# Wide bf16 filler matmuls behind the first layer's second and third norm and at the end of every pass

## The chip, the cores and the metric

The kernel runs on one core of a Trainium2 chip, in one launch. The metric is the device time in microseconds. Three runs of the kernel before took 2702.28, 2705.74 and 2709.91 us (median 2705.74). TensorE's matmul side is called PE in the profile, its weight loads PEld; DVE is VectorE, ACT ScalarE, POOL GpSimd, SP the engine that issues the transfers.

## The reference, cut to what matters

Four layers are applied one after the other to `x` of 32 sequences, 128 tokens and 128 features, with a context of the same shape:

- layer 0: a transformer decoder block, 16 heads of 64: causal self attention, residual and layer norm (`ln1`); cross attention to the context, residual and layer norm (`ln2`); feed-forward of 512 with relu, residual and layer norm (`ln3`);
- layer 1: a small attention with 16 heads of 8, masked per query;
- layer 2: an encoder block and a decoder block with linear attention, 8 heads of 16;
- layer 3: a small attention, a norm and projection to `U`, then a recurrence over the 128 tokens, `s = silu(s @ A.T) + u_t`, whose states are projected and added to the result.

```python
x = _layer_norm(ca + residual, ln2_g, ln2_b)
residual = x
h = jax.nn.relu(x @ ffn_w1 + ffn_b1)
x = _layer_norm(h @ ffn_w2 + ffn_b2 + residual, ln3_g, ln3_b)
```

## The kernel before, in words

**Passes.** The 32 sequences are worked on in 8 passes of 4 (`G = 4`, `GT = 512` tokens). In each pass a main stream computes layer 0 of its four sequences, and a side stream computes layers 1 to 3, up to `U`, of the four sequences of the pass before. Pass 0 has set-up work in place of the side stream. After pass 7 the side stream runs once alone (about 2313 to 2582 us of the span), and then the recurrence of all 32 sequences runs in one scan of 127 steps, to 2702 us.

**Order.** Every engine has its own program, written by the same generators: `MAIN_STEPS` is the list of the main stream's steps, and `interleave` (called from `passes`, line 423) takes one main step and then as many side steps as `SIDE_PACE` says are due. So the order on each engine is fixed, and an engine that waits holds up all that is behind it, of both streams. The main steps at the end of a pass are

```python
steps += [[("ln2", "y")], [], [], [("ln2", "norm")], [("ln2", "n")], []]
steps += [[("ffn", 0), ("ffn", 1)], [("ffn", 2), ("ffn", 3)], []]
steps += [[("ln3", "y")], [], [], [("ln3", "norm")], [("ln3", "n")]]
```

**A norm.** Item `y`: PE sums the projection and the residual into PSUM bank 0 (`sums`, line 654, matmuls of line 660). DVE takes the moments (lines 1159 to 1165), POOL the power -0.5 (line 546), DVE writes the normalised tokens to `main_normed` in four instructions (`normalise`, line 1172). Item `n`: PE turns them to feature-major with four transposes (`turn4`, line 648), and DVE applies gain and bias (line 1185) into `xT_a` (after `ln2`) or `xT_b` (after `ln3`). After `ln2` come the four feed-forward matmuls (line 652, `ps<-xT_a,w_f`), whose results ACT and DVE take in turn. After `ln3`'s `n`, PE waits until DVE has taken the turned tokens (`wait_emptied`, line 761).

**The hand-over.** DVE then copies `xT_b` to `x_side`, `cT` to `c_side`, makes the side's query mask (lines 1269 to 1272) and the masks of the next pass (lines 1203 to 1209). PE turns the next input (`x_in`), makes the side's first three projections (lines 652 and 800), turns the context (`c_in`) and, once DVE has copied that to `cT` (line 1224), starts the next self attention with `w_qkv_sa`.

**PSUM.** The main stream uses banks 0 to 4, the side stream 5 to 7. Bank 3 holds the attention's outputs (`o`) and one of the value products; it is read out before `ln2`'s `y` begins.

**The matmuls.** fp32 operands take two PE instructions for each matmul of the program; bf16 takes one. `scores` adds the mask with one bf16 matmul of 512 columns (line 698). The scan has a local helper `keep_busy(width)` (line 965) that multiplies `ident_h` (a bf16 identity) with `width` columns of `mask_ca` into bank 5 in each step, 512 or 256 wide.

Of the kernel before, what the change touches and what calls it, by code (L numbers as in the profile page):

```python
# [50 lines left out]
def main_steps():  # L51
# [8 lines left out]
    def attention(tag):  # L60
        for s in range(UNITS + 3):
# [11 lines left out]
            if tag == "sa" and s % 2 and s < 2 * G:  # L73
# [14 lines left out]
MAIN_STEPS = main_steps()  # L88
NO_FILL = ("scale", "norm")
IDLE = 1  # L90


SIDE_PACE = ([8] * (2 + IDLE) + [4] * (SMALL["l1"][0] * G + 2) + [3] * 37
             + [4] * (SMALL["l3"][0] * G + 2) + [4] * 7)
# [154 lines left out]
def build_program(nc, I, out):  # L249
    with ExitStack() as ctx:  # L250
        def sb(name, shape, dt=F32):
            return ctx.enter_context(nc.sbuf_tensor(name, shape, dt))
# [4 lines left out]
        ps = ctx.enter_context(nc.psum_tensor("ps", [128, 8, 512], F32))  # L257
# [3 lines left out]
        ident_h = sb("ident_h", [128, 128], BF16)  # L261
# [40 lines left out]
        mask_ca = sb("mask_ca", [128, G, T], BF16)  # L302
# [92 lines left out]
        def bank(st, name):  # L395
            return ps[:, st.bank[name], :]
# [5 lines left out]
        def wait_emptied(eng, i, st, name):  # L402

            by = st.by[name]
            eng.wait_ge(emptied[st, by], i.at(st.total[by], st.rank[name]))
# [8 lines left out]
        def wait_all_emptied(eng, i, st, names):  # L414

            last = {}
            for name in names:
                by = st.by[name]
                last[by] = max(last.get(by, 0), st.rank[name])
            for by, rank in last.items():  # L420
                eng.wait_ge(emptied[st, by], i.at(st.total[by], rank))
# [77 lines left out]
        def _(pool):  # L499
# [63 lines left out]
            def side(i):  # L563
# [22 lines left out]
                yield  # L586
                for _ in range(IDLE):
                    yield
# [50 lines left out]
        def _(pe):  # L639
            mm = nc.tensor.matmul  # L640
            pe.wait_ge(consts_ready, n_const[0])
            pe.wait_ge(loaded_first, n_first[0])
            nc.tensor.transpose(ps[:, 5, 0:NCOLS], col_rows[:, :], ident[0:NCOLS, 0:NCOLS]).then_inc(setup_filled, 1)

            def turn4(st, name, src):

                for b in range(G):
                    last = nc.tensor.transpose(bank(st, name)[:, b * 128:b * 128 + 128], src(b), ident[:, :])  # L648
                last.then_inc(filled[st], 1)

            def one(st, name, lhs, rhs):
                mm(bank(st, name)[0:lhs.shape[-1], :], lhs, rhs, start=True, stop=True).then_inc(filled[st], 1)  # L652
# [14 lines left out]
            def token(x, b):  # L667
                return x[:, b * T:b * T + T]

            def before_filling(i, item, *needed):  # L670

                held = [MAIN.before[item]] if MAIN.before[item] is not None else []
                wait_all_emptied(pe, i, MAIN, held + list(needed))

            def project(i, item):
                tag, kind, n = item[:3]
                x = {"sa": xT["a"], "ca": xT["b"] if kind == "q" else cT}[tag]
                if item == ("ca", "v", 0, 0):
                    pe.wait_ge(loaded_ca, n_ca[0])

                needed = {("sa", "k", 0): [("in", 0), ("in", 1)], ("ca", "q", 0): [("ln1", "n")]}
                before_filling(i, item, *needed.get(item, []))
                if kind == "v":
                    one(MAIN, item, token(x, item[3]), w_qkv[tag][:, 2, n * 512:n * 512 + 512])
                else:
                    one(MAIN, item, w_qkv[tag][:, "qk".index(kind), n * 128:n * 128 + 128], x[:, :])

            def scores(i, item):

                tag, _, u = item  # L690
                c, b0 = u // 2, 2 * (u % 2)
                before_filling(i, item, (tag, "k", c), (tag, "q", c))
                for n in range(2):
                    at = slice((b0 + n) * T, (b0 + n) * T + T)
                    mm(bank(MAIN, item)[:, n * 256:n * 256 + 256], queries[:, c % 2, at], keys[:, c % 2, :, at],  # L695
                       start=(n == 0), stop=False, skip_group_check=True)
                mask = (mask_sa if tag == "sa" else mask_ca)[:, b0:b0 + 2, :]
                mm(bank(MAIN, item), ident_h[:, :], mask.unsqueeze(2).broadcast_to([128, 2, 2, T]),  # L698
                   start=False, stop=True, skip_group_check=True).then_inc(filled[MAIN], 1)

            def turn(i, item):
                tag, _, u = item
                before_filling(i, item)
                pe.wait_ge(scaled, i.at(2 * UNITS, u + 1 + (0 if tag == "sa" else UNITS)))
                for h in range(4):
                    last = nc.tensor.transpose(bank(MAIN, item)[:, h * 128:h * 128 + 128],  # L706
                                               probs[:, u % 3, h * 128:h * 128 + 128], ident[:, :])
                last.then_inc(filled[MAIN], 1)
# [14 lines left out]
            def main(i):  # L723
                for step in MAIN_STEPS:
                    for item in step:
                        tag, kind = item[:2]
                        if tag == "in":

                            if kind == 0:
                                pe.wait_ge(group_in, i.at(48, 48))  # L730
                            turn4(MAIN, item, lambda b: (c_in if kind else x_in)[:, b, :])
                        elif tag == "ffn":
                            before_filling(i, item, ("ln2", "n"))
                            one(MAIN, item, w_f1[:, kind * 128:kind * 128 + 128], xT["a"][:, :])
                        elif kind in ("q", "k", "v"):
                            if item == ("sa", "v", 0, 0):

                                pe.wait_ge(masks_taken, i.at(1, 1))
                            project(i, item)
                        elif kind == "s":  # L740
                            scores(i, item)
                        elif kind == "t":
                            turn(i, item)
                        elif kind == "o":
                            outputs(i, item)
                        elif kind == "y":
                            pe.wait_ge(main_residual_ready, i.at(3, MAIN_LN.index(tag) + 1))
                            if tag == "ln3":
                                before_filling(i, item, *[("ffn", c) for c in range(FC0)])
                                sums(MAIN, tag, lambda b: [(token(hidden[:, c, :], b), w_f2[:, c, :]) for c in range(FC0)]  # L750
                                     + [(token(main_residual, b), ident[:, :])])
                            else:
                                t = "sa" if tag == "ln1" else "ca"
                                before_filling(i, item, *[(t, "o", u) for u in range(UNITS)])
                                sums(MAIN, tag, lambda b: [(token(headsT[:, c, :], b), w_o[t][:, c, :]) for c in range(C0)]
                                     + [(token(main_residual, b), ident[:, :])])
                        elif kind == "n":
                            before_filling(i, item, (tag, "y"))
                            turn4(MAIN, item, lambda b: main_normed[:, b, :])
                            if tag == "ln3":  # L760
                                wait_emptied(pe, i, MAIN, item)
                    yield

# [42 lines left out]
            def side(i):  # L806
# [6 lines left out]
                yield  # L813
                for _ in range(IDLE):
                    yield
# [95 lines left out]
            def setup_side():  # L911
# [19 lines left out]
                yield  # L931

            passes(pe, main, side, setup_side())


# [26 lines left out]
                if j == sum(FINAL_GROUPS[n]) - 1:  # L962
                    last.then_inc(fin_mm, 1)

            def keep_busy(width):

                mm(ps[:, 5, 0:width], ident_h[:, :], mask_ca[:, :, :].rearrange("p g t -> p (g t)")[:, 0:width],
                   start=True, stop=True)

            for k in range(1, T):  # L970
                scan_step(k)
                if k >= FINAL_STEPS and k % FINAL_STEPS == 0:
                    final_states(k // FINAL_STEPS - 1)
                elif k >= FINAL_STEPS and k % FINAL_STEPS == 1:
                    final_residual(k // FINAL_STEPS - 1)
                    keep_busy(256)
                else:
                    keep_busy(512)
            pe.wait_ge(scan_silu, T - 1)
            final_states(FINAL_BLOCKS - 1)  # L980
            final_residual(FINAL_BLOCKS - 1)
# [3 lines left out]
        def _(act):  # L985
# [62 lines left out]
            def side(i):  # L1048
                take(i, SIDE, ("l1", "k"), k0[:, :], ACT.Relu, bias=v1("L1_xattn_bk"), scale=1.0)
                yield  # L1050
                yield
                for _ in range(IDLE):
                    yield
# [49 lines left out]
        def _(dve):  # L1103
# [194 lines left out]
            def side(i):  # L1298
# [9 lines left out]
                yield  # L1308
                for _ in range(IDLE):
                    yield  # L1310
# [118 lines left out]
```

## Time and profile before

| what | value |
|---|---|
| median of three runs | 2705.74 us |
| the profiled execution's own time | 2704.2 us |
| its span, first to last instruction | 2702.5 us |
| mean granted TensorE clock | 0.904 of full speed |
| PE busy | 2301.2 us, 85% |
| PE weight loads busy | 1569.6 us, 58% |
| DVE busy | 1479.7 us, 55% |
| ACT busy | 1171.4 us, 43% |
| POOL busy | 341.4 us, 13% |

Busy times are shares of the span of one execution. The granted clock is the share of full speed (2.4 GHz) that the chip lets TensorE run at; 0.50 is 1.2 GHz. A mean between the two over a stretch tells how much of it was spent at either level.

### The profile page before, as it was taken

Reading aid. Unit: us, or ns where it says so; the run is one execution under the profiler, and the core shown is the slowest. Engines: PE = TensorE matmul, PEld = TensorE weight load, DVE = VectorE, ACT = ScalarE, POOL = GpSimd, SP = SyncE. Lnnn points to the kernel's source line nnn. Section 1 sums busy time; section 2 is a strip of 40 time slices with the busy share of each in tenths; the row PEclk is TensorE's granted clock in tenths of the full one; section 3 lists DMA queues with packets and bytes.
Section 4 is the critical chain, followed back from the end, with each engine's and each line's share of the span. In section 5 each row is a group of like instructions: output and inputs, shape, how many; then the busy total and the mean of one; then the engine's idle time right before and its main releaser. Section 6 shows DMA issues by size and latency. Waiting matters only on the chain.

```text
span 2702.5 us, 31506 instructions
## 1 busy us (share of the span) xinstructions
PE 2301.2 (85%) x11045; PEld 1569.6 (58%) x11053; DVE 1479.7 (55%) x3864; ACT 1171.4 (43%) x4001; POOL 341.4 (13%) x351
## 2 busy tenths in 40 slices
PE   6887988898888988898888988898889888785789
PEld 3554655666565655566565656565566656453456
DVE  4554666565756666466746666566656575333210
ACT  3452635364544635273535545363536454121111
POOL 1002012110112011201201011201111011201100
PEclk9988999999999999899999999999989999656555
DMA  5000000000000000000000000000000000000000
GB/s 154 1 1 13 1 1 1 5 10 1 1 1 13 1 1 1 13 1 1 1 1 13 1 1 1 13 1 1 1 5 1 1 1 1 0 0 0 0 12 20
DMA packets 25122, 19.85 MB, mean 7 GB/s; under 512 B 2243, under 2 KB 22790, under 8 KB 24966
## 3 DMA queue, kind: packets, MB, share of 16 engines
q1 hardware_dynamic: 24966, 17.83, 2.4%
q8 instruction: 90, 1.47, 0.2%
q14 instruction: 66, 0.54, 0.1%
HBM read 15.73 MB, written 2.10 MB: 7 GB/s over the span
## 4 chain that ended last, share of the span: by engine, by line
PE 64%; DVE 21%; ACT 7%; issue 4%; POOL 3%; SPq 0%; DMA 0%; POOLq 0%; DVEq 0%
PE ps L652 14%; PE ps L660 8%; PE ps L793 7%; PE ps L695 7%; PE ps L718 6%; PE ps L776 4%; PE ps L786 4%; DVE tok L1172 3%; PE ps L706 3%; ACT probs L999 3%; DVE keys L1239 2%; PE ps L648 2%; DVE stats L1159 2%; PE ps L942 2%; POOL kx L569 2%
## 5 line engine op out<-in xcount | busy, mean ns | idle before, releaser
L999 ACT ACTIVATE probs<-ps,neg_max 128x128 f32<-128x128 f32 x1024 | 362.7, 367 | 422.1 <-DVE neg_max L1152 415.5
L999 ACT ACTIVATE s_probs<-ps,s_max 128x128 f32<-128x128 f32 x768 | 219.5, 368 | 275.1 <-DVE s_max L1152 275.0
L695 PE MATMUL ps<-keys,queries 128*128 128x256 f32 x1024 | 282.3, 399 | 28.4 <-ACT queries L993 28.4
L718 PE MATMUL ps<-probsT,values 128*128 128x256 f32 x1024 | 277.2, 394 | 3.7 <-ACT headsT L1033 2.7
L793 PE MATMUL ps<-kx,qT 32*128 32x512 f32 (+1 forms) x384 | 244.0, 718 | 34.9 <-POOL kx L569 34.9
L1152 DVE TENSOR_REDUCE neg_max<-ps 128x4 f32<-128x512 f32 x256 | 176.8, 691 | 165.2 <-PE ps L698 163.8
L1152 DVE TENSOR_REDUCE s_max<-ps 128x4 f32<-128x512 f32 x192 | 132.7, 691 | 235.7 <-PE ps L793 233.6
L695 PEld LDWEIGHTS ps<-keys,queries 128*128 128x128 f32 x1024 | 187.9, 195 | 120.0 <-ACT queries L993 42.3
L546 POOL TENSOR_TENSOR rstd<-var_eps,minus_half 128x4 f32<-128x4 f32 x88 | 90.4, 1028 | 1239.1 <-DVE var_eps L1165 1238.3
L1159 DVE BATCH_NORM_STATS2 stats<-ps 128x6 f32<-128x128 f32 x352 | 78.3, 285 | 297.8 <-PE ps L660 294.2
L718 PEld LDWEIGHTS ps<-probsT,values 128*128 128x128 f32 x1024 | 178.3, 194 | 66.7 <-issue 24.8
L999 ACT ACTIVATION_READ_ACCUMULATOR probs<-ps,neg_max 128x1 f32 x1024 | 208.6, 204 | 0.0
L706 PEld LDWEIGHTS ps<-ident,probs 128*128 128x128 f32 x1024 | 124.0, 142 | 129.3 <-issue 83.4
L993 ACT ACTIVATE probsT<-ps 128x512 f32<-128x512 f32 x256 | 156.0, 609 | 49.6 <-PE ps L706 48.3
L776 PEld LDWEIGHTS ps<-l1v,s_probsT 128*128 128x128 f32 x1024 | 143.9, 209 | 51.8 <-issue 49.3
L706 PE MATMUL ps<-ident,probs 128*128 128x128 f32 x1024 | 159.2, 279 | 0.4 <-DVE probs L1195 0.4
L648 PE MATMUL ps<-ident,tok 128*128 128x128 f32 x352 | 60.1, 296 | 103.7 <-DVE tok L1172 90.4
L652 PE MATMUL ps<-xT_a,w_qkv_sa 128*128 128x512 f32 x256 | 132.3, 604 | 12.0 <-DVE cT L1224 10.3
L540 POOL TENSOR_TENSOR pool_scratch<-minus_half 128x1 f32<-128x1 f32 x88 | 17.1, 195 | 988.8 <-DVE x1T L1289 676.1
L786 PE MATMUL ps<-ident,s_probs 128*128 128x128 f32 x768 | 133.1, 300 | 10.5 <-ACT s_probs L999 8.8
L776 PE MATMUL ps<-l1v,s_probsT 128*128 128x9 f32 x1024 | 137.1, 261 | 0.7 <-ACT s_probsT L993 0.7
L1254 DVE COPY headsT<-ps 64x256 f32<-64x256 f32 x256 | 107.6, 420 | 39.7 <-PE ps L718 37.6
(207 smaller groups left out, 4031.6 us busy)
## 6 DMA issues: line engine op xcount, KB each, us to landing
x_in<-in_x SPq DMA_DIRECT2D x8, 256.0 KB, 3.0
c_in<-in_ctx SPq DMA_DIRECT2D x8, 256.0 KB, 3.2
skip_in<-in_mask_BxS_ik SPq DMA_DIRECT2D x8, 256.0 KB, 3.3
out<-headsT SPq DMA_DIRECT2D x28, 64.0 KB, 1.8
valid_in<-in_mask_BxS_bf SPq DMA_DIRECT2D x8, 64.0 KB, 3.4
w_qkv_sa<-in_L_xattn_sa_wq SPq DMA_DIRECT2D x1, 512.0 KB
w_qkv_sa<-in_L_xattn_sa_wk SPq DMA_DIRECT2D x1, 512.0 KB
w_qkv_sa<-in_L_xattn_sa_wv SPq DMA_DIRECT2D x1, 512.0 KB
```

The source lines that it names most:

```text
L652: mm(bank(st, name)[0:lhs.shape[-1], :], lhs, rhs, start=True, stop=True).then_inc(filled[st], 1)
L660: last = mm(dst, l, r, start=(n == 0), stop=(n == len(todo) - 1))
L695: mm(bank(MAIN, item)[:, n * 256:n * 256 + 256], queries[:, c % 2, at], keys[:, c % 2, :, at], start=(n == 0), stop=False, skip_group_chec ...
L706: last = nc.tensor.transpose(bank(MAIN, item)[:, h * 128:h * 128 + 128], probs[:, u % 3, h * 128:h * 128 + 128], ident[:, :])
L718: last = mm(bank(MAIN, item)[:, n * 256:n * 256 + 256], values[:, c // 4, b0 + n, (c % 4) * 128:(c % 4) * 128 + 128], probsT[:, u % 2, n * ...
L776: last = mm(bank(SIDE, (tag, "o", b))[:, at:at + d1], s_probsT[:, u % 2, h * 128:h * 128 + 128], value[:, b, q * 4 + h, :], start=True, st ...
L786: last = nc.tensor.transpose(bank(SIDE, (tag, "t", u))[:, h * 128:h * 128 + 128], s_probs[:, u % 2, h * 128:h * 128 + 128], ident[:, :])
L793: mm(bank(SIDE, (tag, "s", s)), qT[part, b * T:b * T + T], kx[part, :, b * T:b * T + T], start=True, stop=True).then_inc(filled[SIDE], 1)
L993: A(dst, view(s) if view else s, fn, **kw).then_inc(emptied[st, "A"], 1)
L999: last = A(dst[:, u % dst.shape[1], h * 128:h * 128 + 128], bank(st, (tag, "s", u))[:, h * 128:h * 128 + 128], ACT.Exp, bias=src_max[:, u ...
L1152: V.tensor_reduce(dst[:, u % 2, :], bank(st, (tag, "s", u)).rearrange("p (h k) -> p h k", h=4), AX.X, ALU.max, negate=True).then_inc(max_r ...
L1159: last = V.bn_stats(stats[:, slot, b, :], bank(st, (tag, "y"))[:, b * 128:b * 128 + 128])
```

## The change

The scan's helper is replaced by one that is defined at the top of the tensor program and takes a count of 256-column halves and a bank: it issues bf16 matmuls of `ident_h` with `ident_h`, repeated along the columns, 512 wide (two halves) or 256 wide (a last single half), each with `start` and `stop`, with no wait and no semaphore. `keep_busy(16, 3)` is eight matmuls of 512 columns into bank 3, `keep_busy(12, 3)` six. Eight are issued ahead of the wait for `main_normed` in item `n` of `ln2` and of `ln3`, and six between `ln3`'s turn and the wait behind it. So each of the 8 passes has 22 more bf16 matmuls and their weight loads. In the scan the number and the width of the fillers stay (512 and 256); their moving operand is now the repeated identity.

```diff
+BUSY = {"ln2": 16, "ln3": 16, "end": 12}
...
+            def keep_busy(halves, unused=0):
+
+                for n in range(0, halves, 2):
+                    width = 256 * min(2, halves - n)
+                    mm(ps[:, unused, 0:width], ident_h[:, :], ident_h[:, :].unsqueeze(1).broadcast_to([128, width // 128, 128]),
+                       start=True, stop=True)
...
                         elif kind == "n":
+                            if tag in BUSY:
+                                keep_busy(BUSY[tag], 3)
                             before_filling(i, item, (tag, "y"))
                             turn4(MAIN, item, lambda b: main_normed[:, b, :])
                             if tag == "ln3":
+                                keep_busy(BUSY["end"], 3)
                                 wait_emptied(pe, i, MAIN, item)
...
-            def keep_busy(width):
-
-                mm(ps[:, 5, 0:width], ident_h[:, :], mask_ca[:, :, :].rearrange("p g t -> p (g t)")[:, 0:width],
-                   start=True, stop=True)
-
...
-                    keep_busy(256)
+                    keep_busy(1, 5)
                 else:
-                    keep_busy(512)
+                    keep_busy(2, 5)
```

## Rows read from the trace of the kernel before

**Rows 1.** The page, part 4: the chain that ended last, by engine

```profile
PE 64%; DVE 21%; ACT 7%; issue 4%; POOL 3%; SPq 0%; DMA 0%; POOLq 0%; DVEq 0%
```

**Rows 2.** The page, part 2: granted TensorE clock in 40 equal slices

```profile
PEclk9988999999999999899999999999989999656555
```

**Rows 3.** Windows, second norm to third, passes 0 to 3: busy by engine, PEclk

```profile
219.20:236.60 17.40, 11.28 (x52) 7.21 (x52) 5.12 (x18) 1.38 (x2) 2.77 (x3) 0.79 0.00 0
514.40:530.80 16.40, 13.76 (x64) 8.50 (x64) 8.85 (x33) 2.06 (x3) 3.79 (x4) 0.90 0.00 0
810.70:827.40 16.70, 13.71 (x64) 8.19 (x64) 8.99 (x34) 2.06 (x3) 3.79 (x4) 0.90 0.01 1
1109.20:1126.80 17.60, 14.92 (x64) 9.15 (x64) 8.89 (x33) 2.06 (x3) 3.79 (x4) 0.81 0.01 1
```

**Rows 4.** Windows, third norm to the next pass's first scores, passes 0 to 3

```profile
236.60:254.50 17.90, 13.74 (x37) 7.15 (x38) 9.87 (x20) 3.34 (x5) 12.15 (x11) 0.73 0.19 49
530.80:548.60 17.80, 12.03 (x37) 5.76 (x37) 12.11 (x22) 3.34 (x5) 12.12 (x11) 0.90 0.16 48
827.40:845.50 18.10, 12.80 (x37) 6.35 (x37) 11.75 (x22) 3.34 (x5) 12.07 (x11) 0.81 0.16 47
1126.80:1145.40 18.60, 13.29 (x37) 6.79 (x37) 11.82 (x22) 3.34 (x5) 12.14 (x11) 0.82 0.17 46
```

**Rows 5.** Windows inside pass 1's stage behind the second norm

```profile
515.00:516.00 1.00, 0.12 (x1) 0.15 (x2) 0.74 (x3) 0.00 (x0) 0.00 (x0) 1.00 0.00 0
516.00:519.00 3.00, 2.85 (x10) 1.97 (x10) 2.08 (x10) 0.00 (x0) 1.28 (x2) 0.52 0.00 0
```

**Rows 6.** Timeline, pass 1, second norm: start, us, engine, line, what [idle before]

```profile
512.55 1.13 PE L652 MATMUL ps<-kx,turned 128*128 128x512 f32 x2 [0.69 <-ACT kx L993]
...
515.88 0.91 PE L648 MATMUL ps<-ident,main_normed 128*128 128x128 f32 x4 [2.21 <-DVE main_normed L1172]
...
517.79 4.78 PE L652 MATMUL ps<-xT_a,w_f 128*128 128x512 f32 x8
```

**Rows 7.** Timeline, pass 1: a bf16 mask matmul and the next

```profile
549.50 0.38 PE L698 MATMUL ps<-mask_sa,ident_h 128*128 128x512 bf16 x1
...
549.71 1.02 PE L652 MATMUL ps<-xT_a,w_qkv_sa 128*128 128x512 f32 x2
```

**Rows 8.** Timeline, pass 1: sums into one bank, with their loads

```profile
509.14 1.87 PEld L660 LDWEIGHTS ps<-w_o_ca,headsT 128*128 128x128 f32 x16
509.25 1.95 PE L660 MATMUL ps<-w_o_ca,headsT 128*128 128x128 f32 x16
```

**Rows 9.** Timeline, pass 1, third norm and hand-over

```profile
532.35 0.63 PE L648 MATMUL ps<-ident,main_normed 128*128 128x128 f32 x4 [1.42 <-DVE main_normed L1172]
...
534.24 0.81 DVE L1185 TENSOR_SCALAR xT_b<-ps,col_all 128x512 f32<-128x512 f32 x1
...
535.11 0.66 PE L648 MATMUL ps<-ident,x_in 128*128 128x128 f32 x4 [2.13 <-DVE xT_b L1185]
...
541.45 0.68 DVE L1224 COPY cT<-ps 128x512 f32<-128x512 f32 x1
...
542.28 1.96 PE L652 MATMUL ps<-xT_a,w_qkv_sa 128*128 128x512 f32 x4 [1.03 <-DVE cT L1224]
```

**Rows 10.** Timeline, pass 0: the turn of the second norm and the next input

```profile
220.71 1.09 PE L648 MATMUL ps<-ident,main_normed 128*128 128x128 f32 x4 [4.22 <-DVE main_normed L1172]
...
240.09 1.12 PE L648 MATMUL ps<-ident,x_in 128*128 128x128 f32 x4 [0.90 <-DVE xT_b L1185]
```

**Rows 11.** Line 648 by tile: ns min/median/max of one transpose

```profile
L648 PE MATMUL ps<-ident,main_normed x96: 272/273/447, 119.0 to 2314.5; 128*128 128x128 f32 x96
```

**Rows 12.** Windows: the scan

```profile
2585.00:2700.00 115.00, 111.93 (x430) 80.83 (x436) 5.69 (x9) 23.71 (x124) 0.00 (x0) 0.50 0.09 18
```

**Rows 13.** Line 698 by tile: ns min/median/max of a load and a matmul

```profile
L698 PEld LDWEIGHTS ps<-mask_ca,ident_h x128: 97/98/151, 123.3 to 2270.8; 128*128 128x128 bf16 x128
L698 PE MATMUL ps<-mask_ca,ident_h x128: 379/379/634, 123.5 to 2271.1; 128*128 128x512 bf16 x128
```

## The prediction

> **What bounds the kernel now.** I read the chain of waits first: PE holds 64% of it, DVE 21%, ACT 7% [rows 1]. So time that PE's work takes is mostly time of the kernel, and TensorE's clock sets that. Next the slices: the granted clock is full in most of the first 33 slices with a dip about every four of them, and about half in the last ones, where the side stream and the scan run alone [rows 2]. A pass is some 295 us or four and a half slices, so the dips belong to a place in the pass. The windows by stage find it. From the second norm to the third the mean clock is 0.90 in passes 1 and 2 and 0.81 in pass 3 [rows 3]; from there to the next pass's first scores it is 0.90, 0.81 and 0.82 [rows 4]. (Passes 4, 5 and 6 repeat 1, 2 and 3 within 0.1 us, and 7 repeats 1.) The clock has two levels, 1.2 and 2.4 GHz, so a stretch of T us with mean clock m spent 2(1-m)T at half: 3.3, 3.3 and 6.7 us behind the second norm, 3.6, 6.9 and 6.7 us behind the third. The small windows and the timeline show one such fall: PE ends at 513.7, idles 2.21 us for DVE's `main_normed`, starts the turn at 515.88, and from about 516 to past 519 it is at 1.2 GHz, exactly when it has the turn and the feed-forward matmuls to do [rows 5, 6].
>
> **What a fall costs.** Two prices, from passes that differ in it. Behind the second norm, pass 3 has 3.4 us more at half than pass 1 and is 1.2 us longer [rows 3]: 0.35 us for each us at half. A check by instructions in pass 1: the turn takes 0.91 us there and 0.63 in the third norm [rows 6, 9], 0.28 more; the first feed-forward matmul, two instructions of 0.43 us at full clock (half of the 1.02 us pair of [rows 7] less its tail), takes twice that at half, 0.85 more; 1.13 us together, against 0.35 x 3.3 = 1.15. Behind the third norm the passes give (18.6-17.8)/3.1 = 0.26 and (18.1-17.8)/3.3 = 0.09 [rows 4], since DVE's mask work lies on the way there; I take 0.2.
>
> **The gain, if the clock stays at 2.4 GHz in both stages.** Second norm, passes 1 to 7: 2(3.3+3.3+6.7)+3.3 = 29.9 us at half, x 0.35 = 10.5 us. Pass 0 has no side stream and idles 4.22 us there [rows 10]; the fillers cover the first 1.7 us of it only, so I count 0.5 us. Hand-over, passes 1 to 6: 2(3.6+6.9+6.7) = 34.4 us, x 0.2 = 6.9; pass 7, 0.7 like pass 1; pass 0 has 9.7 us at half [rows 4], worth 1.9 at that price, of which I count 1. Together 19.6 us.
>
> **What the fillers cost.** A bf16 matmul of 512 columns that is followed at once holds PE for 549.71-549.50 = 0.21 us [rows 7]; alone it takes 0.38 [rows 13]. These are the two bounds of one filler. I take 0.21, since a run of sixteen fp32 matmuls into one bank, each with its weight load, goes through in 1.95 us though a load or matmul alone takes longer than the 0.12 between them: loads and matmuls of one run overlap, same bank or not [rows 8]. At 0.21 and a tail of 0.17 (0.38-0.21):
> - Second norm: 8 x 0.21 + 0.17 = 1.9 us, in a gap of 2.21 [rows 6]. Cost 0; what hides it is DVE's normalise. 0.3 us is left.
> - Third norm: 1.9 us in a gap of 1.42 [rows 9], so the turn comes 0.45 us later. It ended at 532.98, but DVE, busy with the side's last two outputs, takes it at 534.24 [rows 9]: 1.26 us of cover, cost 0. Without the side stream (pass 0) the gap is as long as at the second norm, 4.22, by the same chain.
> - Pass end: 6 x 0.21 + 0.17 = 1.4 us, from about 533.4 to 534.8; PE had idled until `xT_b` was done at 535.05 [rows 9]. Cost 0. In pass 0 the gap is only 0.90 [rows 10], so once 0.5 us.
> - Bank 3 has been read out and the fillers have no semaphore: nothing waits for them but what is behind them on PE. The scan's fillers keep number and width; the mask matmul already reads a repeated operand [rows 7], cost 0.
>
> At half clock a filler takes twice as long, 3.4 us for eight, and would be 1.2 us late at the second norm; this needs a fall before it begins.
>
> **What is late next.** With the clock up, PE ends the hand-over's side projections up to 1.8 us sooner (half of 3.6), but the next projection waits for `cT`, which DVE gives only some 0.7 us sooner. The gap ahead of `w_qkv_sa`, now 1.03 us [rows 9], grows to about 2.1, as long as the one after which the clock fell at the second norm. No filler is put there. A fall of 3.4 us would hit work on which PE is the bound, for at most 3.4/2 = 1.7 us. I take one pass in three: 7 x 1.7 / 3 = 4 us given back.
>
> **The sum.** 19.6 - 0.5 - 4 = 15 us. The profiled execution takes 2704.2 us, so 2689; the median of the runs is 1.5 us above it, so 2691. About 0.3% (8 us) is what a measurement of this kernel can tell from no change.
>
> **Two rules against it.** Transposes take 447 ns at the slow end and 272 at the median [rows 11], and the slow ones are those that ran at half clock [rows 6, 9]. The Trainium skill ("TensorE: Matmul & The Clock Gate", Part 4) says that the full clock does not engage for transposes; by that the turn's 0.28 us would not be gained in 16 turns, and the sum would be 10.5 instead of 15. The trace disagrees: they run at either level.
> In [rows 8] each load lasts into the matmul before it. The same page (Part 3) says that a load overlaps with matmuls in flight only when the row group differs; here all take the whole array. What that would do to the fillers is the last rival below.
>
> **Rivals.**
> - *The fall comes anyway later in the hand-over*, in every pass instead of one in three. For: the 2.1 us gap, and that nothing fills it. Against: the projections ahead of it run densely. 19.6 - 0.5 - 7 x 1.7 = 7 us: 2698.5, on either side of the 0.3% bound. Chance 0.16.
> - *The fillers do not hold the clock*, so the change does not do what it says; all is hidden, and the time stays at 2706. For: in the scan PE is busy 112 of 115 us with a filler in every step, and is at 0.50 all the time [rows 12]. Against: there each filler stands alone between small matmuls that wait for ACT, at a clock that was down when it began; here eight follow one another at full clock. Chance 0.14.
> - *The fillers are longer than the gaps.* If each weight load (0.10 us, [rows 13]) is added to its matmul, a filler is 0.31 us, eight are 2.65 with the tail: 0.45 us late at the second norm; at the third 1.25 late, just covered; the six at the end then start near 534.2 and end at 536.2, 1.1 late. 1.55 x 7 + 1 = 12 us. With the clock held this leaves 2703; with the falls as before it is 2718, slower. It decides from (2.21-0.17)/8 = 0.255 us a filler on. Against: [rows 7, 8]. Chance 0.07.
> - My forecast: 0.63.
>
> **The range.** Without any give-back the sum is 19 us, and with the dips elsewhere in the pass falling luckier or worse by some 3 us (an estimate: two stretches of half clock at 1.7 us), 2683. Upwards 2702 takes in most of the second case and leaves out the fillers that do nothing and those that are too long. Faster by over 0.3%: 0.63 less a few hundredths for small gains, and half of 0.16, together 0.69; within 0.3%: 0.24; slower 0.07.
>
> **What would show it.** Windows over the stage behind the second norm at clock 1.00 in nearly all of passes 1 to 7, and the stage 1.1 us shorter in passes 1, 2 and 2.2 in pass 3; the turn there at 0.63 us; each filler 0.21 us from the last; idle ahead of `main_normed`'s turn near 0.3 us and not replaced by lateness; the hand-over 0.7 to 1.5 us shorter. Wrong would be: clock still below 0.95 in these stages, the turn starting more than 1.6 us after normalise begins, or new falls at `w_qkv_sa` in most passes.

## The result, and the profile after

| | before | changed |
|---|---|---|
| median | 2704.54 us (4 runs) | 2681.01 us (4 runs) |
| profiled execution | 2704.2 us, span 2702.5 | 2683.9 us, span 2682.2 |
| mean granted clock | 0.904 | 0.917 |
| PE busy | 2301.2 us | 2310.2 us |

The ratio is 0.9899, 95% interval 0.9867 to 0.9932: 18 to 36 us faster. Three of the changed kernel's runs took 2672.26, 2678.13 and 2683.88 us; the fourth, at 8943.78 us, was disturbed and is not in the ratio, but it counts in the median of four. The median of the other three is 2678.13 us. So the gain is 24 us by the medians of four and 26 without the disturbed run, where 15 were forecast, and the time lies 2 to 5 us under the range, which began at 2683.

The slices of the page, and the chain by engine, answer to [rows 1, 2]:

```profile
PEclk9989999999999999999999999999999999656555
PE 63%; DVE 23%; ACT 7%; issue 4%; POOL 3%; SPq 0%; DMA 0%; POOLq 0%; DVEq 0%
```

The dips inside the passes have gone from the slices, but for the one in pass 0; the half clock of the last ones is as it was. The windows by stage of the changed kernel, second norm to third in passes 0 to 3, answer to [rows 3], column by column (PEclk third from the end):

```profile
220.50:238.20 17.70, 13.32 (x60) 8.13 (x60) 5.11 (x18) 1.38 (x2) 2.77 (x3) 0.81 0.00 0
513.30:528.80 15.50, 13.28 (x70) 8.04 (x69) 9.01 (x33) 2.06 (x3) 3.79 (x4) 1.00 0.00 0
807.70:823.20 15.50, 13.27 (x70) 8.07 (x69) 8.97 (x34) 2.06 (x3) 3.79 (x4) 1.00 0.00 1
1100.20:1115.70 15.50, 13.28 (x70) 8.09 (x69) 8.97 (x34) 2.06 (x3) 3.79 (x4) 1.00 0.00 1
```

and those from the third norm to the next scores, passes 0 to 3, to [rows 4]:

```profile
238.20:253.40 15.20, 11.31 (x42) 5.73 (x43) 9.68 (x20) 3.34 (x5) 10.65 (x10) 1.00 0.19 57
528.80:545.70 16.90, 13.20 (x51) 6.38 (x50) 12.09 (x22) 3.34 (x5) 11.17 (x11) 1.00 0.18 51
823.20:840.10 16.90, 13.21 (x52) 6.38 (x51) 12.12 (x22) 3.34 (x5) 11.22 (x11) 1.00 0.17 51
1115.70:1132.60 16.90, 13.22 (x52) 6.38 (x51) 12.11 (x22) 3.34 (x5) 11.23 (x11) 1.00 0.20 51
```

Passes 4 to 6 are the same within 0.1 us, at 1.00 too. In passes 1 to 6 the clock is 1.00 in both stages and all passes are alike: 15.5 us where they had been 16.4 to 17.6, 16.9 where they had been 17.8 to 18.6. Pass 7's second norm is the same; in its hand-over the clock is 0.81. Pass 0 still has a fall behind its second norm. The timeline of pass 1, to be read against [rows 6, 9], shows the fillers (line 650) in their gaps:

```profile
511.51 1.13 PE L660 MATMUL ps<-kx,turned 128*128 128x512 f32 x2 [0.69 <-ACT kx L999]
512.48 1.89 PE L650 MATMUL ps<-ident_h 128*128 128x512 bf16 x8
514.85 0.63 PE L656 MATMUL ps<-ident,main_normed 128*128 128x128 f32 x4 [0.49 <-DVE main_normed L1178]
...
516.48 3.92 PE L660 MATMUL ps<-xT_a,w_f 128*128 128x512 f32 x8 [0.56 <-DVE xT_a L1191]
...
528.76 1.89 PE L650 MATMUL ps<-ident_h 128*128 128x512 bf16 x8
530.49 0.60 PE L656 MATMUL ps<-ident,main_normed 128*128 128x128 f32 x4
530.93 1.46 PE L650 MATMUL ps<-ident_h 128*128 128x512 bf16 x6
532.29 0.81 DVE L1191 TENSOR_SCALAR xT_b<-ps,col_all 128x512 f32<-128x512 f32 x1
533.15 0.66 PE L656 MATMUL ps<-ident,x_in 128*128 128x128 f32 x4 [0.77 <-DVE xT_b L1191]
...
538.52 0.68 DVE L1230 COPY cT<-ps 128x512 f32<-128x512 f32 x1
539.35 1.96 PE L660 MATMUL ps<-xT_a,w_qkv_sa 128*128 128x512 f32 x4 [1.75 <-DVE cT L1230]
```

Eight fillers take 1.89 us, 0.216 each and a tail. The turn takes 0.63 us instead of 0.91, the feed-forward matmuls 3.92 instead of 4.78, and DVE still begins `xT_b` 1.2 us after the later turn has ended.

**Where the 20.3 us of span went.** Differences of starts in the two timelines (a stage begins with normalise on DVE, the middle of a pass with its first scores):

| part | before | after | gained |
|---|---|---|---|
| second norm to third, passes 1 to 7 | 16.45, 16.62, 17.58, 16.45, 16.61, 17.58, 16.45 | 15.49 each | 9.3 |
| third norm to scores, passes 1 to 6 | 17.80, 18.16, 18.61, 17.79, 18.16, 18.60 | 16.86 each | 8.0 |
| pass 0, both stages | 17.39 + 17.88 | 17.70 + 15.25 | 2.3 |
| middle of passes 1 to 7 | 259.91, 262.10, 263.72, 259.88, 262.09, 263.71, 259.89 | 259.93, 262.00, 260.14, 261.44, 262.02, 260.15, 261.45 | 4.2 |
| pass 0 to its second norm | 219.20 | 220.46 | -1.3 |
| lone side stream with its hand-over | 269.27 | 271.48 | -2.2 |
| scan | 120.5 | 120.5 | 0 |

The middle holds no filler and yet changed, in some passes by 3.6 us. It was read next.

### The profile page after: what moved, and what is told of

It reads as the page before. It is cut to its first block, busy times and chain, and to the rows that moved or that the text cites. A ratio compares the mean times of both kernels' runs of the same rounds, so it can differ in the third digit from the quotient of the medians.

```text
span 2682.2 us, 31866 instructions
## 1 busy us (share of the span) xinstructions
PE 2310.2 (86%) x11229; PEld 1574.6 (59%) x11229; DVE 1481.0 (55%) x3864; ACT 1171.2 (44%) x4001; POOL 342.4 (13%) x351
## 4 chain that ended last, share of the span: by engine, by line
PE 63%; DVE 23%; ACT 7%; issue 4%; POOL 3%; SPq 0%; DMA 0%; POOLq 0%; DVEq 0%
PE ps L660 12%; PE ps L668 9%; PE ps L804 7%; PE ps L703 7%; PE ps L726 6%; PE ps L787 4%; PE ps L797 4%; DVE tok L1178 3%; ACT probs L1005 3%; PE ps L714 3%; DVE keys L1245 2%; DVE stats L1165 2%; POOL kx L570 2%; PE ps L953 2%; PE ps L656 2%
## 5 line engine op out<-in xcount | busy, mean ns | idle before, releaser
L1165 DVE BATCH_NORM_STATS2 stats<-ps 128x6 f32<-128x128 f32 x352 | 78.2, 285 | 297.0 <-PE ps L668 293.5
L797 PE MATMUL ps<-ident,s_probs 128*128 128x128 f32 x768 | 133.0, 300 | 10.5 <-ACT s_probs L1005 8.8
```

What stands on the lines that cost most here:

```text
L797: last = nc.tensor.transpose(bank(SIDE, (tag, "t", u))[:, h * 128:h * 128 + 128], s_probs[:, u % 2, h * 128:h * 128 + 128], ident[:, :])
L1165: last = V.bn_stats(stats[:, slot, b, :], bank(st, (tag, "y"))[:, b * 128:b * 128 + 128])
```

## The experiments

All are edits of the changed kernel.

**1. The same kernel once more, for the falls at `w_qkv_sa`.** No edit.

> The changed kernel itself, once more and timed in more rounds. The first profile of it showed no fall of the clock at w_qkv_sa after the hand-over in any of seven passes, though the gap ahead of it is 1.75 us. Theory A (those falls do not come, because the projections ahead of the gap are dense): again none in seven passes, each hand-over stage (third norm to the first scores) within 0.1 us of 16.86 us. Rival B (it was luck of where the falls happened to land): one or more of the seven passes shows 1.2 GHz at w_qkv_sa and a stage about 1 to 1.7 us longer. Either way the time is 2672 to 2686 us; the spread between runs is 5 to 12 us if the falls in the rest of a pass land differently from run to run.

2679.59 us, ratio to the kernel before 0.9907 (0.9892 to 0.9922), runs 2678.83 to 2683.91. Passes 1 to 6 took 16.85 to 16.87 us from the third norm to the scores: again no fall in any, though everything lay elsewhere in time (its third norm of pass 1 began at 524.05 us, 528.84 in the first profile). So rival B is out; the spread was 5 us. With both profiles that is 12 hand-overs without the fall that I had in one of three. The reason that theory A gives for it, the dense projections ahead of the gap, was not tested apart.

**2. Only the second norm's fillers.**

```diff
-BUSY = {"ln2": 16, "ln3": 16, "end": 12}
+BUSY = {"ln2": 16, "ln3": 0, "end": 0}
```

> Only the eight fillers of the second norm. If each group of fillers saves what its own stage shows, the stage behind the second norm is 15.5 us in passes 1 to 7 (before 16.45, 16.62, 17.58) and the hand-over keeps its falls: 17.8 to 18.6 us from the third norm to the first scores. Time 2704.5 - 9.3 = 2695 us, give or take 4 for falls elsewhere. Rival: a fall behind the second norm is only moved on into the feed-forward or the third norm, then that stage stays near 16.4 us and the time near 2704.

2696.28 us, ratio 0.9971 (0.9959 to 0.9983). The stage is 15.48 us in all of passes 1 to 7, as expected, and the time is near the 2695. But the way there is another: the profile's gain of 8 us was made in pass 0, most of it ahead of the first filler, and in the two passes behind it. From then on a pass took 296.95 us, as long as the mean pass before. The stage was 1.4 us shorter than its mean before, the hand-over 18.4 us instead of 18.2 and the middle 263.0 instead of 261.9, so all of the saving was given back outside the stage. In the clock's records a pass of the kernel before has 20.5 us at half on the mean, and so has each of these: 3.4 us more of it in the middle than before. The window over the middle of pass 5:

```profile
1430.47:1693.50 263.03, 235.38 (x1222) 164.94 (x1221) 162.42 (x426) 137.45 (x476) 26.03 (x26) 0.97 0.00 1
```

**3. Only the fillers of the third norm and of the end.**

```diff
-BUSY = {"ln2": 16, "ln3": 16, "end": 12}
+BUSY = {"ln2": 0, "ln3": 16, "end": 12}
```

> Only the eight fillers of the third norm and the six of the pass's end. The stage behind the second norm stays at 16.4 to 17.6 us with the clock near 0.90, the one behind the third norm is 16.9 us (before 17.8, 18.2, 18.6) at clock 1.00 in passes 1 to 6. Time 2704.5 - 8 - 2.6 (pass 0) = 2694 us, give or take 4. Together with the second norm's alone the two gains should add up to the whole; if one group makes the other needless, each alone gives nearly all of it, below 2688.

2674.93 us, ratio 0.9894 (0.9875 to 0.9913): not 2694, but no slower than the whole change. The stages are what was expected, 16.45 and 16.86 us, so the second norm's fall is back in every pass, and costs nothing in the mean pass (293.49 us here, 293.55 in the changed kernel). The gains of the two groups do not add up.

**4. Thin fillers.** The same places and number, 8 columns instead of 512.

```diff
+            def keep_thin(count, unused):
+                for n in range(count):
+                    mm(ps[:, unused, 0:8], ident_h[:, :], ident_h[:, 0:8], start=True, stop=True)
...
-                                keep_busy(BUSY[tag], 3)
+                                keep_thin(BUSY[tag] // 2, 3)
...
-                                keep_busy(BUSY["end"], 3)
+                                keep_thin(BUSY["end"] // 2, 3)
```

> The same 22 fillers in the same places, each 8 columns wide instead of 512, so PE is given the instructions and weight loads but hardly any streaming. If it is the work of the wide fillers that holds the clock, the falls are back as before the change (clock 0.90 and 0.81 in both stages, stages 16.4 to 17.6 us and 17.8 to 18.6 us) and the time is 2700 to 2708 us. Rival: what holds the clock is that PE issues anything in the gap, or its weight loads; then it is near 2681 us with the stages at clock 1.00.

2709.03 us (one run). Its windows, second norm and hand-over of passes 1 and 2, have the clock and the lengths of [rows 3, 4]:

```profile
517.60:534.00 16.40, 13.78 (x66) 8.59 (x67) 8.82 (x33) 2.06 (x3) 3.79 (x4) 0.90 0.00 0
534.00:551.80 17.80, 12.35 (x51) 6.40 (x50) 12.14 (x22) 3.34 (x5) 12.14 (x11) 0.90 0.18 49
815.50:833.10 17.60, 14.96 (x68) 9.37 (x68) 8.88 (x34) 2.06 (x3) 3.79 (x4) 0.81 0.00 0
833.10:851.80 18.70, 13.71 (x52) 7.32 (x51) 11.85 (x22) 3.34 (x5) 12.14 (x11) 0.82 0.15 46
```

So matmuls and weight loads as such do not hold the clock. But thin fillers also leave the gap nearly as idle as it was, as the second norm of pass 1 shows: eight take 0.34 us, and PE then waits 2.03 us.

```profile
516.70 0.34 PE L656 MATMUL ps<-ident_h 128*128 128x8 bf16 x8
519.07 0.71 PE L661 MATMUL ps<-ident,main_normed 128*128 128x128 f32 x4 [2.03 <-DVE main_normed L1183]
```

Whether it is the width of the fillers or only the time that they fill was therefore not told apart; for that, narrow matmuls would have to fill the whole gap, and no run has them.

**5. Without the end's six, and 6. with them alone.**

```diff
-BUSY = {"ln2": 16, "ln3": 16, "end": 12}
+BUSY = {"ln2": 16, "ln3": 16, "end": 0}
...
-BUSY = {"ln2": 16, "ln3": 16, "end": 12}
+BUSY = {"ln2": 0, "ln3": 0, "end": 12}
```

> The changed kernel without the six fillers at the pass's end. What is to be told apart: in the runs so far passes 1 to 7 took 296.97 us on average before and with the second norm's fillers alone (296.95), and 293.5 us both in the whole change and in the one with the third norm's and the end's fillers alone, though the stage behind the second norm differs by 1 us between the last two. Theory A (a pass settles on one of these two lengths, and a saving too small to reach the next is given back as a fall elsewhere): mean pass 293.5 or 296.9, nothing between, and a span near 2677 or 2695. Rival B (every group of fillers brings its own saving): the hand-over shows falls in part of the passes, a mean pass of 294 to 295.5 us and a span of 2680 to 2690.

> Only the six fillers at the pass's end (none at either norm). Theory A: a mean pass of 293.5 or 296.9 us, most likely 296.9, as the falls behind the second norm and ahead of the third norm's turn remain. Rival B: the hand-over keeps about half of its falls, mean pass near 295.5, span near 2692.

2684.56 and 2683.88 us (one run each). Without the end's fillers the hand-over still takes 16.82 us, with them alone 16.84: either group keeps the clock up there, so none of rival B's part falls appeared. The last passes are 293.54 us long in both. By the length of a pass that is theory A; the spans, 2682.8 and 2682.2 us, are not the 2677 that it named, because of pass 0 (see below), and the first lies within B's 2680 to 2690. My guess that the six alone would leave 296.9 was wrong.

Experiment 5 shows one thing more. In pass 1 of the kernel before, the clock fell at 536.6 us, 1.5 us behind PE's wait of 2.13 us for `xT_b` [rows 9]. Here that wait is 2.02 us, and the clock does not fall in the hand-over of any of passes 1 to 6:

```profile
533.84 0.66 PE L656 MATMUL ps<-ident,x_in 128*128 128x128 f32 x4 [2.02 <-DVE xT_b L1191]
```

So the length of one gap does not tell whether a fall follows.

**7. Twelve fillers more in each pass.** In each pass PE waits 3.1 us for POOL's spread keys before the side stream's last small attention (line 888 of the kernel before). Behind that wait the clock was at half for 6.8 us in each of passes 1 to 7 of every profile so far.

```diff
-                pe.wait_ge(keys_ready, i.at(3, 3))
                 wait_emptied(pe, i, SIDE, ("l3", "v"))
                 wait_emptied(pe, i, SIDE, ("l3", "q"))
+                keep_busy(24, 6)
+                pe.wait_ge(keys_ready, i.at(3, 3))
```

> The changed kernel, and twelve fillers of 512 columns more in each pass, where PE waits 3.1 us for POOL's spread keys of the small attention of layer 3 (bank 6, whose last contents have been read by then); behind that wait every pass has 1.2 GHz for 6.8 us in every kernel so far. If that fall goes, 0.35 us for each us at half gives 2.4 us a pass. Theory A: with 2.4 us and the 1 us that the second norm's fillers save without showing it, the mean pass goes from 293.5 to about 290.1 us, 3.4 less, 24 us in all: near 2655 us. Rival B: 2.4 us a pass, 17 us in all, 2662. Rival C: the fill only moves the fall to the next gap, 2679.

2654.40 us, ratio 0.9818 (0.9802 to 0.9835), and the mean pass 290.13 us. Theory A had said 2655 and 290.1, rival B 2662 and rival C 2679. The same place in the changed kernel and in this one (PEclk 0.72 and 1.00):

```profile
457.00:469.00 12.00, 8.91 (x24) 4.98 (x23) 4.11 (x7) 5.21 (x21) 4.30 (x3) 0.72 0.00 0
```

```profile
452.00:464.00 12.00, 11.13 (x49) 6.43 (x47) 5.98 (x11) 6.65 (x23) 2.14 (x2) 1.00 0.00 0
```

**8. Twice the fillers in each place.**

```diff
-BUSY = {"ln2": 16, "ln3": 16, "end": 12}
+BUSY = {"ln2": 32, "ln3": 32, "end": 24}
```

> Twice the fillers in each of the three places (16, 16 and 12 of 512 columns), more than the gaps take. At 0.21 us each: second norm 3.6 us in a gap of 2.4, 1.3 us late; third norm 3.6 in 1.4, 2.2 late, of which 1.3 is hidden by DVE; pass end 2.7 us from then on, which ends about 2.6 us after x_in could start. The stages behind the norms get 1.2 and about 3 us longer than with the single fillers, at clock 1.00: 16.7 us and 19.5 to 20 us. If passes settle on one of few lengths, the mean pass is 296.97 or 300.4 us; if not, 293.5 + 4 = 297.5.

2696.66 us (one run). The second norm's stage is 16.54 us (expected 16.7), the hand-over 17.45, where 19.5 to 20 was expected: PE's side projections then follow `x_in` without a gap and take the lateness up, and `cT` on DVE decides as before. Together 1.6 us longer than with the single fillers; the mean pass is 3.4 longer, 296.97. Its timeline of pass 3, where the 16 fillers at the third norm and the 12 at the end leave no idle time:

```profile
1118.86 3.62 PE L650 MATMUL ps<-ident_h 128*128 128x512 bf16 x16
1122.32 0.60 PE L656 MATMUL ps<-ident,main_normed 128*128 128x128 f32 x4
1122.75 2.75 PE L650 MATMUL ps<-ident_h 128*128 128x512 bf16 x12
1125.34 0.60 PE L656 MATMUL ps<-ident,x_in 128*128 128x128 f32 x4
```

**The lengths of a pass.** The rows below are the start of the third norm's normalise, pass 1 and pass 7, six passes apart: first the kernel before, then the changed one, then the one of experiment 3.

```profile
530.83 1.37 DVE L1172 TENSOR_SCALAR main_normed<-ps,meanvar,rstd 128x128 f32<-128x128 f32 x4 [1.12 <-POOL rstd L546]
2312.62 1.37 DVE L1172 TENSOR_SCALAR main_normed<-ps,meanvar,rstd 128x128 f32<-128x128 f32 x4 [1.12 <-POOL rstd L546]
```

```profile
528.84 1.37 DVE L1178 TENSOR_SCALAR main_normed<-ps,meanvar,rstd 128x128 f32<-128x128 f32 x4 [1.12 <-POOL rstd L547]
2290.11 1.37 DVE L1178 TENSOR_SCALAR main_normed<-ps,meanvar,rstd 128x128 f32<-128x128 f32 x4 [1.12 <-POOL rstd L547]
```

```profile
521.86 1.37 DVE L1178 TENSOR_SCALAR main_normed<-ps,meanvar,rstd 128x128 f32<-128x128 f32 x4 [1.12 <-POOL rstd L547]
2282.81 1.36 DVE L1178 TENSOR_SCALAR main_normed<-ps,meanvar,rstd 128x128 f32<-128x128 f32 x4 [1.12 <-POOL rstd L547]
```

(2312.62-530.83)/6 = 296.97 us, (2290.11-528.84)/6 = 293.55, (2282.81-521.86)/6 = 293.49. In this way, for all profiles but that of the thin fillers:

| mean pass | kernels |
|---|---|
| 296.95 to 296.97 | before; second norm only, passes 4 to 7 (296.41 over all six); twice the fillers |
| 293.5 to 293.6 | changed; again; third norm and end; no end; end only; experiment 9 |
| 290.12 to 290.13 | experiments 7, 10 and 11 |

The thin fillers gave 297.3 over these six. Single passes differ: before they repeated 294.9, 296.5 and 299.45, in the changed kernel 292.5, 293.8 and 294.4, in the kernel of experiment 3 each one was 293.4 to 293.5. What fills a pass up is a fall. In the changed kernel it comes in some passes in the output sums of the cross attention (2.02 us at full clock in pass 1, 3.65 after a fall in pass 2):

```profile
502.11 2.02 PE L668 MATMUL ps<-w_o_ca,headsT 128*128 128x128 f32 x16 [1.04 <-DVE headsT L1260]
```

```profile
794.85 3.65 PE L668 MATMUL ps<-w_o_ca,headsT 128*128 128x128 f32 x16 [1.04 <-DVE headsT L1260]
```

Pass 0 is another matter. Its second norm began at 212.7 to 221.5 us in the thirteen profiles, though no filler lies ahead of it there, and at 215.9 and 220.5 us in the two of the changed kernel. So the times of single runs (experiments 4, 5, 6 and 8) do not tell less than some 9 us apart; the mean pass does.

**9. Fillers where the clock is half all the time.** Behind each step of the lone side stream, and two instead of one in the scan.

```diff
-            passes(pe, main, side, setup_side())
+            interleave(main(Pass(0)), setup_side(), [1] * SETUP_STEPS)
+            for g in range(1, GROUPS):
+                interleave(main(Pass(g)), side(Pass(g - 1)))
...
+            for _ in side(Pass(GROUPS - 1)):
+                keep_busy(24 if n_steps == 0 else 6 if n_steps in small else 12, 0)
+                n_steps += 1
...
-                    keep_busy(2, 5)
+                    keep_busy(4, 5)
```

> The changed kernel with fillers where the clock is half all the time: behind each step of the last, lone side stream (bank 0; 3 of 512 columns behind a step of the small attentions, 6 elsewhere, 12 behind the first) and two instead of one of 512 in most steps of the scan. No fillers of this kind could hold the clock in the scan before (a filler in every step, PE busy 112 of 115 us, clock 0.50). If it is a matter of how much wide work PE gets: the scan's clock rises to 1.00 after its first steps and a step takes about 0.65 instead of 0.91 us, 30 us less, and the small attentions' steps go from 5.1 to about 3.8 us, 30 us less; 2620 to 2640 us. If fillers hold a clock that is up but do not bring it back, the scan stays at 0.50, its steps get longer (PE has 0.85 us of fillers at half clock, about 1.0 us a step) and the time is 2690 to 2700 us.

2655.73 us, ratio 0.9822 (0.9804 to 0.9840). The scan did what the first theory says, 120.5 us became 91.6; the lone side stream did not, 271.5 became 275.8. The windows, first the scan, then the first small attention:

```profile
2575.00:2645.00 70.00, 69.26 (x409) 40.29 (x408) 4.71 (x7) 19.48 (x102) 0.00 (x0) 1.00 0.12 23
2303.00:2398.00 95.00, 95.00 (x283) 55.86 (x282) 20.02 (x37) 22.56 (x69) 1.74 (x2) 0.50 0.00 1
```

In the second PE is busy every microsecond and is at 1.2 GHz. The clock fell in the attention's second step and three fillers a step did not bring it back; a step took 5.85 us, 5.07 without fillers. The scan found the clock up: it had risen in the lone side stream's last steps, 13 us before the scan began at 2558.2 us. So this run shows that two fillers a step hold the clock in the scan, not that they raise it.

**10. The two that gained, together.** Experiment 7's edit and the scan's.

> The changed kernel with the twelve fillers ahead of POOL's spread keys and with two fillers of 512 columns in most steps of the scan, the two edits that gained alone (2654 us and 29 us of the scan). They lie in different parts of the time, so they should add up: mean pass 290.1 us, scan 92 us, 2654 - 29 = 2625 us.

2630.30 us, ratio 0.9729 (0.9709 to 0.9750). They add up, but for 5 us: here the scan began at 1.2 GHz, the clock rose 9 us into it, and the profiled scan took 94.6 us. This run is the one in which two fillers a step bring the clock back:

```profile
2530.50:2539.60 9.10, 9.10 (x36) 6.59 (x36) 0.00 (x0) 1.63 (x9) 0.00 (x0) 0.50 0.00 0
2539.80:2620.00 80.20, 79.36 (x468) 46.39 (x468) 5.36 (x8) 22.04 (x116) 0.00 (x0) 1.00 0.12 24
```

**11. More for the small attentions.** As 10, and in the lone side stream

```diff
...
+            first_l3 = SIDE_STEPS - 7 - SMALL["l3"][0] * G - 2
...
+            for _ in side(Pass(GROUPS - 1)):
+                keep_busy(24 if n_steps == 0 else 16 if n_steps in (3, 4, first_l3, first_l3 + 1) else 10 if n_steps in small else 12, 0)
+                n_steps += 1
```

> As keys_scan, and the lone side stream with five fillers of 512 columns behind each step of the small attentions (eight behind their first two) and six elsewhere. With three the attentions stayed at half clock (a step 5.85 us) after a fall in their second step. If more wide work is what they lack, the step goes to 3.8 to 4.0 us at full clock, 26 steps, 30 to 40 us less than with three, 25 to 30 less than keys_scan: 2595 to 2600 us. If the attentions' own work (32 rows, 9 columns) keeps it down anyway, the steps become 6.7 us at half clock and the time is 2640 us or more.

2578.89 us, ratio 0.9536 (0.9516 to 0.9557), 16 us under the lower end of what was expected. Mean clock 0.992, lone side stream 222.9 us instead of 271.5. Windows over it and over the scan, and a step of the attention, 3.67 us long:

```profile
2270.00:2345.00 75.00, 73.48 (x372) 42.48 (x371) 22.21 (x40) 24.29 (x74) 11.54 (x10) 0.98 0.00 1
2345.00:2490.00 145.00, 132.08 (x695) 75.90 (x693) 56.94 (x191) 25.04 (x62) 21.56 (x21) 0.99 0.00 1
2490.00:2578.00 88.00, 83.93 (x493) 48.79 (x491) 5.69 (x9) 23.48 (x123) 0.00 (x0) 1.00 0.12 25
```

```profile
2291.96 1.12 PE L804 MATMUL ps<-kx,qT 32*128 32x512 f32 x2
2293.02 1.25 PE L650 MATMUL ps<-ident_h 128*128 128x512 bf16 x5
2294.11 0.95 PE L787 MATMUL ps<-l1v,s_probsT 128*128 128x9 f32 x8
2295.05 0.66 PE L797 MATMUL ps<-ident,s_probs 128*128 128x128 f32 x4
```

## Why the prediction was wrong in its size

**The mechanism** was right at each place where fillers were put: the clock is 1.00 in both stages of passes 1 to 7 but for the last hand-over, the turn takes 0.63 us, the fillers lie in their gaps, and without their 512 columns the falls are back (experiment 4). All three rivals are out: the fillers hold the clock, they are not too long, and the fall later in the hand-over came in none of 12.

**The terms.** Second norm, passes 1 to 7: 10.5 forecast, 9.3 measured, or 0.31 us for each us at half instead of 0.35; 0.96, 1.13 and 2.09 us by pass where 1.15, 1.15 and 2.3 were meant. The last 0.2 us is DVE's: it takes the feed-forward's last result only behind the side stream's normalise. Hand-over, passes 1 to 6: 6.9 forecast, 8.0 measured, 0.23 us for each us at half instead of 0.2. Pass 7's hand-over: 0.7 forecast, not seen; its clock was 0.81 and it lies in the part that lost 2.2 us. Pass 0: 1 net forecast, 2.3 measured; the 0.5 us for its end was too little to see in that. Fillers: 0.21 us meant, 0.216 measured; the three costs of nothing were nothing, with the covers that were named (0.49 us of idle time left at the second norm, 1.2 us of DVE's work at the third). The Trainium skill ("TensorE: Matmul & The Clock Gate", Part 3) says that a load overlaps with matmuls in flight only when the row group differs. These fillers all take the whole array, and eight took 1.89 us, not the 2.65 of loads that do not overlap.

**The step that failed** is the one of what is late next: "I take one pass in three: 7 x 1.7 / 3 = 4 us given back". PE's wait for `cT` did grow, from 1.03 to 1.75 us and not to 2.1, and the clock fell behind it in none of 12 hand-overs. The forecast took the length of a gap as the sign of a fall, and experiment 5 shows that it is none. The second step that failed is that the rest of a pass would stay as it was, but for 3 us of luck: the middle of the passes, where no filler lies, gave 4.2 us in the profile. Together these are 8 us; pass 0's beginning and the lone side stream lost 3.5, and what is left is near the 5 us by which the profile's gain of 20.3 exceeds the sum.

**The reason behind it** is that the sum adds stages, and the stages do not add. Once they had settled, the passes had, falls included, one of three mean lengths, 3.4 us apart. A saving in one stage was spent on a fall in another (experiment 2: none of the stage's 1.4 us a pass arrives; experiment 3: leaving out the 0.96 us costs nothing), and then one more saving moved the passes by 3.4 us each (experiment 7), where its own price was 2.4. The change as a whole is such a step: 6 x 3.42 = 20.5 us of its gain lie between the third norms of passes 1 and 7, as two single groups of it, third norm or end, do alone. So of the savings that the sum added up, the settled passes took 0 or 3.4 us each and nothing between. The whole time is less strict, since pass 0 and the first passes behind it differ too (experiment 2 gained 8 us in this way). That the mean lengths are steps is shown by twelve profiles; why a fall comes just where a pass would otherwise be too short is not shown, and I give no mechanism for it. That the number came as near as it did was luck in part: two errors of about 4 us in one direction met 3.5 us of loss that was not counted either.

**The reading of the scan** as evidence against the change was too strong. Fillers do work there, only one of 512 columns in each step was too few; with two, the clock rose from 0.50 to 1.00 within the scan (experiment 10) and stayed there (experiments 9 to 11).

## What to carry to other kernels

Look for stretches with a granted clock of 0.5 before looking for busy time, the longest first (here the tail, not the passes), and put independent wide bf16 matmuls in the gaps ahead of the work that suffers: an attention step went from 5.07 to 3.67 us though PE had looked full. In a loop whose body repeats, do not sum small savings: measure the mean period over many turns, since it may move in steps.

## What the runs showed of the hardware that I had not expected

- The mean pass, once settled, was 296.97, 293.5 or 290.13 us in all kernels but one, in steps of 3.4 us, whatever was saved or added in single stages (0.96 us added: none; 1.6 us added: 3.4; one fall of 6.8 us taken out: 3.4).
- The clock can be brought back from 1.2 to 2.4 GHz and kept there by wide matmuls whose results nobody reads, in a chain of small dependent steps: a scan step went from 0.91 to 0.69 us (experiment 10).
- PE can be busy all the time and stay at 1.2 GHz. Attention matmuls of 32 rows or 9 columns with three fillers a step stayed at 0.50 with PE 100% busy; eight fillers in the first two steps and five in the others kept 0.98. Which of the two, the stronger start or the fuller steps, did it was not tried apart.
- Transposes run at both levels, 0.63 us for four at 2.4 GHz and 1.09 at 1.2. The Trainium skill ("TensorE: Matmul & The Clock Gate", Part 4) says that the full clock does not engage for them; these runs disagree.
